# Softmax shifts of eight heads turned at once and put into the query stack by DMA, second attention pass thirteen heads behind the first

## What is computed

```python
xn = _adaln(x, cond, ln1_w, ln1_b)
q, k, v = split(xn @ qkv_w.T);  q, k = _rope(q), _rope(k)
x = x + _attn(q, k, v) @ sa_out_w.T              # layer 0: attention to itself
xn = _adaln(x, cond, ln2_w, ln2_b)
q = _rope(xn @ q_w.T);  k = _rope(ctx @ k_w.T);  v = ctx @ v_w.T
x = x + _attn(q, k, v) @ ca_out_w.T              # layer 1: attention to a context
xn = _adaln(x, cond, ln3_w, ln3_b)
x = x + gelu(xn @ ffn_w1.T + ffn_b1) @ ffn_w2.T + ffn_b2
# _attn: softmax(q k^T / sqrt(32)) v for each head
```

## Time and profile before

| what | value |
|---|---|
| median of 3 runs | 1967.09 us (1962.93 to 1968.1) |
| the profiled execution's own time | 1963.51 us |
| its span, first to last instruction | 1961.7 us |
| mean granted TensorE clock | 0.990 |
| PE busy | 1902.3 us, 97% |
| ACT, DVE, POOL busy | 1458.3, 1418.4, 783.0 us |
| attention block | from 0 to about 1278 us; first scores at about 50 us |
| feed-forward block | from about 1280 us to the end |

### The profile page before, as it was taken

The page is one execution under the profiler, slowest core; times in us unless marked ns, Lnnn a source line. Parts: engine busy times, 40 slices in busy tenths (PEclk is TensorE's granted clock), DMA queues, the critical chain, the costliest instruction groups (busy, mean ns, idle before and its releaser), DMA issues. The chain is left out here.

```text
span 1961.7 us, 39861 instructions
## 1 busy us (share of the span) xinstructions
PE 1902.3 (97%) x13588; PEld 1653.0 (84%) x13588; DVE 1418.4 (72%) x2509; ACT 1458.3 (74%) x4005; POOL 783.0 (40%) x820
## 2 busy tenths in 40 slices
PE   7899999999999999999999998899999999999999
PEld 6688888888887888888888877678899989898998
DVE  5777778778777887887887877645666666766654
ACT  3688888888888888888888888745666565665654
POOL 4334334334334444454453442013535354454531
PEclk9899999999999999999999999999999999999999
DMA  7867776876778677778778777343322313233130
GB/s 221 221 174 196 186 188 167 202 184 170 200 201 231 166 214 216 189 202 218 184 205 217 184 206 183 94 156 108 97 92 71 108 55 114 71 97 97 54 97 33
DMA packets 300197, 307.33 MB, mean 157 GB/s; under 512 B 15840, under 2 KB 253792, under 8 KB 300000
## 3 DMA queue, kind: packets, MB, share of 16 engines
q1 hardware_dynamic: 299408, 304.45, 57.4%
q10 hardware_dynamic: 592, 0.34, 0.1%
HBM read 212.46 MB, written 92.27 MB: 155 GB/s over the span
## 5 line engine op out<-in xcount | busy, mean ns | idle before, releaser
L738 ACT ACTIVATE ps_s<-ps_s,neg_max 128x256 f32<-128x256 f32 x1024 | 459.3, 451 | 85.1 <-DVE neg_max L853 81.6
L853 DVE TENSOR_REDUCE neg_max<-ps_s 128x2 f32<-128x512 f32 x512 | 352.7, 690 | 162.7 <-PE ps_s L607 158.8
L752 ACT ACTIVATE prob<-ps_s 128x512 f32<-128x512 f32 x512 | 304.6, 595 | 61.4 <-PE ps_s L627 58.1
L923 POOL TENSOR_TENSOR rope_c<-rope_c,rope_s 128x256 f32<-128x256 f32 x128 | 98.6, 770 | 425.2 <-DVE rope_s L834 425.2
L627 PE MATMUL ps_s<-qT,kT 104*128 104x256 f32 x1024 | 213.8, 291 | 21.0 <-ACT ps_s L738 6.4
L607 PE MATMUL ps_s<-kT,qT 96*128 96x256 f32 x1024 | 218.0, 295 | 10.7 <-DMA qT<-q_turned 5.4
L597 PE MATMUL ps_g<-xx_hi,w_hi 128*128 128x256 f32 x1024 | 214.3, 291 | 7.3 <-DVE rope_s L834 3.4
L607 PEld LDWEIGHTS ps_s<-kT,qT 96*128 96x128 f32 x1024 | 172.3, 193 | 54.8 <-ACT ps_s L738 19.4
L738 ACT ACTIVATION_READ_ACCUMULATOR ps_s<-ps_s,neg_max 128x1 f32 x1024 | 213.7, 209 | 0.0
L627 PEld LDWEIGHTS ps_s<-qT,kT 104*128 104x128 f32 x1024 | 168.8, 193 | 50.6 <-issue 19.4
L597 PE MATMUL ps_g<-xx_hi,w_lo 128*128 128x256 f32 x1024 | 207.6, 285 | 0.0
(11 more groups left out here) (155 smaller groups left out, 4826.9 us busy)
## 6 DMA issues: line engine op xcount, KB each, us to landing
kT<-k_turned SPq DMA_DIRECT2D x192, 256.0 KB, 5.3
qT<-q_turned SPq DMA_DIRECT2D x64, 512.0 KB, 7.3
f_raw<-in_w1T SPq DMA_DIRECT2D x124, 256.0 KB, 3.1
k_turned<-rot_hi SPq DMA_DIRECT2D x64, 256.0 KB, 4.5
k_turned<-rot_lo SPq DMA_DIRECT2D x64, 256.0 KB, 3.0
q_turned<-rot_hi SPq DMA_DIRECT2D x64, 256.0 KB, 4.6
q_turned<-rot_lo SPq DMA_DIRECT2D x64, 256.0 KB, 3.4
qT<-q_turned SPq DMA_DIRECT2D x64, 256.0 KB, 7.8
```

The source lines that it names most:

```text
L738: ins = eng.activation(scores[:, t * L:(t + 1) * L], scores[:, t * L:(t + 1) * L], ACT.Exp, bias=neg_max[G % 2][:, t, j:j + 1], accum_out= ...
L752: eng.activation(prob[:, n % NP, :, :].rearrange("p t l -> p (t l)"), ps_s[:, score_bank(step), :], ACT.Exp).then_inc(exp_done, 1)
L853: eng.tensor_reduce(neg_max[G % 2][:, :, j], ps_s[:, score_bank(step), :].rearrange("p (t l) -> p t l", l=L), AX.X, ALU.max, negate=True). ...
L923: eng.tensor_tensor(rope_c[n % 2][:, 0, :], rope_c[n % 2][:, 0, :], rope_s[:, 0, :], ALU.subtract)
```

## The change

- The turn is made once for eight heads (places 24 G + 24 to + 32 instead of twice per group), and its 16 rows are copied by ACT to a tile of their own, `max_rows`, two of them in turn.
- SP moves them into the query stack: two DMAs per eight heads (`max_rows`), one for the high and one for the low rows, 8 partitions to one partition each. `max_spread` goes away. The key stack needs only two rows of ones there (`ones`, a memset), and `pick` with its two loads goes away.
- LAG grows from 8 to 13. One fewer `prob` buffer is kept (9), and `mix` comes one head sooner after the last `weigh` of its eight.
- The stacks are filled four heads at a time (NQ = 6 places of four instead of 3 of eight), with twice as many DMAs of half the size.
- The copy of projected v from PSUM goes from ACT to DVE.
- In the table the projections of k, q, v and o move: o by 18 places later, q of layer 1 from p + 53 to p + 29 (turns of x there two places later), v from p + 29 and p + 46 to p + 42, and so on.

```diff
-LAG = 8
+LAG = 13
...
-            x_place = p + late + (31 if ahead == B else 16)
+            x_place = p + late + (31 if ahead == B else 18 if B < ahead < N else 16)
...
-                turns(shares((p + 29, 6, k[:4]), (p + 46, 7, k[4:])))
+                turns(spread(p + 29, 13, k))
...
-                    shares((p + 29, 6, v[:4]), (p + 46, 7, v[4:]))
+                spread(*((p + 42, 9, v) if ahead == B else (p + 42, 13, v)))
             if ahead < N - 1:
-                turns(spread(p + 53, 13, q))
+                turns(spread(*((p + 42, 13, q) if ahead < B else (p + 50, 10, q) if ahead == B else (p + 29, 13, q))))
...
-            spread(p + 37, 9, [("project", "o", i - 1, t, c) for cs in (range(KC - 1), (KC - 1,)) for t in range(T) for c in cs])
+            spread(p + 55, 9, [("project", "o", i - 1, t, c) for cs in (range(KC - 1), (KC - 1,)) for t in range(T) for c in cs])
...
-        for half in range(2):
-            put(24 * G + 12 * half + 12, "log", G, half)
-            put(24 * G + 12 * half + 13, "max_split", G, half)
-            put(24 * G + 12 * half + 19, "max_turn", G, half)
-            put(24 * G + 12 * half + 20, "max_copy", G, half)
-            put(24 * G + 12 * half + 23, "max_spread", G, half)
-        if G:
-            put(24 * G - 20, "stack", "k", G)
-            put(24 * G - 17, "stack", "q", G)
+        for n, kind in ((24, "log"), (25, "max_split"), (30, "max_turn"), (31, "max_copy"), (32, "max_rows")):
+            put(24 * G + n, kind, G)
+    for quad in range(2, 4 * N):
+        put(12 * quad - 20, "stack", "k", quad)
+        put(12 * quad - 17, "stack", "q", quad)
...
-        place = 3 * (8 * G + LAG + 9) + 2
+        place = 3 * (8 * G + LAG + 8) + 2
...
-                        if j % OH < 2:
-                            eng.wait_ge(maxes_spread if j % OH else maxes_copied, nth["max_turn", G, j // OH])
...
+                        if n % HG == 0:
+                            G = n // HG
+                            eng.wait_ge(max_rows_in[G % 2], 16 * 2 * (G // 2 + 1))
...
+                    elif kind == "max_rows":
+                        G = step[1]
+                        eng.wait_ge(maxes_copied, G + 1)
+                        if G >= NQ // 2:
+                            eng.wait_ge(weigh_done, HG * (G - NQ // 2 + 1))
+                        first = 2 * G % NQ
+                        for s in range(2):
+                            into = qT[ROWS + s:ROWS + s + 1, first:first + 2, :, :]
+                            eng.dma_start(into.rearrange("p g h l -> p (g h) l").bitcast(F32),
+                                          max_rows[G % 2][s * HG:(s + 1) * HG, :].bitcast(F32)).then_inc(max_rows_in[G % 2], 16)
```

More of the change, by code:

```diff
@@ L165, in stage_order @@
     yield ("warm", WARM_START)
-    yield ("pick",)
+    yield ("ones",)
     for h in range(2):
@@ L217, in stage_order @@
     yield from rotated("q", 0)
-    yield ("stack", "k", 0)
+    for quad in range(2):
+        yield ("stack", "k", quad)
     yield from (step for step in early if step[0] in turns_of_x)
@@ L221, in stage_order @@
     yield from rotated("k", 1)
-    yield ("stack", "q", 0)
+    for quad in range(2):
+        yield ("stack", "q", quad)
     yield from split("v", range(KC), "o")
@@ L384, in block_kernel @@
             total = [sb(f"total{n}", [P, T, HG]) for n in range(2)]
[L385 to L389, removed]
+            log_sb = sb("log_sb", [P, T, HG])
+            shift = sb("shift", [P, T, HG])
+            max_parts = sb("max_parts", [P, T, ROWS])
+            max_rows = [sb(f"max_rows{n}", [2 * HG, L], F32R) for n in range(2)]
+            NP = 9
             prob = sb("prob", [P, NP, T, L])
@@ L741, in attention_scalar @@
                     elif kind == "log":
-                        G, half = step[1:]
-                        eng.wait_ge(total_done, HG * G + OH * (half + 1))
-                        if nth[step] > 2:
-                            eng.wait_ge(shift_done, nth[step] - 2)
-                        eng.activation(log_sb[half][:, :, :], total[G % 2][:, :, OH * half:OH * (half + 1)], ACT.Ln).then_inc(log_done, 1)
+                        G = step[1]
+                        eng.wait_ge(total_done, HG * (G + 1))
+                        if G:
+                            eng.wait_ge(shift_done, G)
+                        eng.activation(log_sb[:, :, :], total[G % 2][:, :, :], ACT.Ln).then_inc(log_done, 1)
                     elif kind == "weigh":
@@ L812, in attention_vector @@
                                           ALU.subtract).then_inc(w_split, 1)
-                    elif kind == "pick":
-                        eng.wait_ge(small_in["pick"], 2 * 16)
-                        for r in range(NG):
-                            for half in range(2):
-                                eng.tensor_copy(kT[ROWS:MROWS, r, OH * half:OH * (half + 1), :],
-                                                pick_sb[ROWS:MROWS, :].unsqueeze(2).broadcast_to([2 * OH, OH, L])).then_inc(picked, 1)
+                    elif kind == "ones":
+                        eng.memset(kT[ROWS:MROWS, :, :, :].bitcast(F32), 1.0).then_inc(ones_set, 1)
                     elif kind == "project" and step[1] in "qk" and step[4] == KC - 1:
@@ L835, in attention_vector @@
                                           ALU.mult).then_inc(rope_taken, 1)
+                    elif kind == "project" and step[1] == "v" and step[4] == KC - 1:
+                        i, t = step[2:4]
+                        eng.wait_ge(product_done, products["v", i, t])
+                        if i >= NV and t == 0:
+                            eng.wait_ge(mix_done, KC * (i - NV + 1))
+                        eng.tensor_copy(v_sb[i % NV][:, t, :], ps_g[:, bank(("project", "v", i, t, 0)), :]).then_inc(v_done, 1)
                     elif kind == "project" and step[1] == "o" and step[4] == KC - 1:
@@ L990, in attention_sync @@
                     elif kind == "stack":
[L991 to L996 removed]
+                        m, quad = step[1:]
+                        i, n = divmod(quad, 4)
+                        eng.wait_ge(spilled[m][n // 2], 32 * (i + 1))
```

143 lines of the change are left out of this document (60 added, 83 removed).

## The result

The changed kernel takes **2096.13 us** (median of 4 runs, 2095.25 to 2096.9), the kernel before 1967.59 us on the same chip (1962.93 to 1969.89). The ratio is **1.0656 [1.0636, 1.0676]**: 6.6% slower, where 1930 us was forecast, with a range from 1904 to 1962. The profiled execution took 2096.90 us, its span is 2095.1 us, its mean granted clock 0.963 (before 0.990).

What follows compares the result with a forecast made beforehand. The prediction took PE, busy 97% of the span, as the bound. It summed -13.4 - 26 - 2 + 5 + 1.5 = -35 us against 1963.5 us to 1928.5, stated as 1930 us, range 1904 to 1962.

Steps and rivals of the forecast that it cites:

- Part 4: New wait of each eight heads' first `weigh` for the row DMAs: 0.08 us for each of 64, +5 us.
- The path of 2.6 + 0.6 + 2.0 = 5.2 us: From turn to rows in the query stack: ACT's copy ends after 2.6, SP's two issues 0.6 apart, landing 2.0 us.
- Time available, 7.4 us: From a turn to its first `weigh`, ten places later: 7.8 us, about 7.4 with the gains on PE.
- The slower rival: Row DMAs on SP's queue land 5.3 us from issue; each first `weigh` waits 1.1 us: 1994 us, chance 0.10.
- Its own sign: Wait of `weigh` on the row DMAs in the profile after: over 40 us in all.
- Part 1: Half of the turns on PE go: 64 pairs of transposes at 0.21 us each, -13.4 us.
- Part 2: ACT and DVE relieved, so PE waits less: half of the possible gain, 10.8 + 5.3 + 10.0, -26 us.
- The 5.3 us at the change of layers: Gain where the layers change, from PE's idle time and lower clock: half of 10.6 us.
- the 10 us of the late stretches: Gain in two late attention stretches, from PE's idle time and lower clock: half of 20.1 us.
- Part 3 and 5: Start, first scores needing four heads' stacks: -2 us; moved steps, five more `weigh` after the last scores: +1.5 us.
- The rule on small loads: Skill page's DMAs of at least 1 MiB: halved stack loads, one by one, would lose some 300 us; given little weight.
- the rival "small loads": Halved stack loads keep the DMA engines busy twice as long, costing 95 us: 2017 us, chance 0.02.

Runs made afterwards that it cites:

- e10: e7 with each max_turn's pair of transposes done twice, 128 more matmuls: 1953.68 us, ratio 0.9938 to the kernel before.
- e1: The change with `weigh` reading 96 rows, so not waiting for the row DMAs; softmax shift left out of the second pass: 1939.43 us, ratio 0.9848.
- e7: The change with the row DMAs issued by ACT instead of SP, both rows in one DMA: 1942.23 us, ratio 0.988 to the kernel before.
- e9: e7 with the statistics of the last x 8 places later: 1937.79 us, ratio 0.9853 to the kernel before.
- e11: e7 with 128 unused reductions of 0.94 us put on DVE at the old spreads' places: 1959.56 us, ratio 0.9958 to the kernel before.
- e5: The change with rows issued by ACT in two DMAs and the copy of v back on ACT: 1945.0 us, ratio 0.9893 to the kernel before.
- e12: e9 with the copy of v back on ACT: 1939.43 us, ratio 0.9853 to the kernel before.
- e6: The kernel before with only the copy of v moved from ACT to DVE: 1959.03 us, ratio 0.9966.

## Why the prediction was wrong

**The failed step is Part 4**: it left SP's time ahead of the rows out of the sum. The stack loads ahead were taken as "mostly through when ACT's copy ends", and of the spill it said: "In layer 0 a spill of q stands just ahead and may hold SP up. I add 0.08 us for each of 64". Neither got a duration, and that a spill of k stands ahead of the rows in layer 1 was not said. In the late cases SP needs 4.6 us of issue and 1.5 us at the spill between turn and rows in layer 0, and 2.5 and 2.2 us in layer 1. SP's stand at this spill was already in the trace of before, where no row DMA stood behind it:

```profile
SPq L987 <- POOL rot_lo L930: 251.2, 108, 5.3
```

The text put a price of 5 us on the whole wait. Measured, the first `weigh` starts some 120 us late in all, 1.9 us for each of 64, or 3.9 us for each of the 31 late ones, and the lower clock behind these waits adds some 56 us of slower matmuls, which the sum had no term for.

What else Part 4 said, by its own steps:

- *The path of 2.6 + 0.6 + 2.0 = 5.2 us* came out near the truth by luck, where SP is free. There, in the even turns of the steady part of layer 0, ACT's copy ends 1.5 us after the turn and not 2.6, and in the four of these turns in which PE waits, it starts 4.0 to 4.2 us after the first issue began, where 0.6 + 2.0 = 2.6 us was forecast: 5.5 to 5.8 us in all. The landing was priced some 1.4 us too low and the copy 1.1 us too high.
- *Time available, 7.4 us*: in the steady parts it is 7.2 us in the odd turns and 5.2 us in the even ones, in both layers, since a turn's ten places hold more or fewer projections. In layer 0 the late rows had the long distance, in layer 1 the short one, where even 4.9 us to the issue was far too late.
- The views shown of SP's order were the place of an even G in layer 0, where a spill stands *behind* the rows. The odd one, 24 places on, has it *ahead*. A step that recurs has to be looked at in each of its positions against the others' period; here that is two groups of eight in an item, in each layer.

**The slower rival** had the right consequence and the wrong mechanism. It said that the rows come late because they "land like the 256 KB loads", at 1.1 us each, all 64 of them, 1994 us. Where PE waits in the steady items it starts 3.2 to 4.4 us after the first of the two issues began, between the 2.6 us of the forecast and the 5.9 us of the rival; the rows are issued late, in 31 of the 64 cases, and by 3.9 us. Its own sign was over 40 us of wait, and 116.3 were found. Its chance, 0.10, was too low for a wait on the path whose DMAs stand in one queue with others that themselves wait.

**Part 1 was right**: 0.18 us measured per pair (e10) against 0.21.

**Part 2 was right in the steady part and not elsewhere.** Without the wait (e1) the change gains 30 us, where all parts but the fourth add up to 40, so the gains were put too high by 10. In e7 the periods are 36.40 us in layer 0 (440.67 less 404.27) and 35.65 in layer 1, forecast near 36.1 in both:

```profile
404.27 0.60 PE L566 MATMUL ps_g<-ident,xn 128*128 128x128 f32 x4
...
440.67 0.60 PE L566 MATMUL ps_g<-ident,xn 128*128 128x128 f32 x4
...
853.70 0.60 PE L566 MATMUL ps_g<-ident,xn 128*128 128x128 f32 x4
...
889.35 0.60 PE L566 MATMUL ps_g<-ident,xn 128*128 128x128 f32 x4
```

The waits on `total` from 112 to 575 us are 7.3 us in e9, half of the 14.8 in the earlier trace rows, as said:

```profile
PEld ps_s L603 <- ACT ps_s L732: 6.6, 16, 0.4
PEld ps_s L622 <- ACT ps_s L732: 0.7, 1, 0.7
```

DVE's part of it is measured by e11, 15 us; ACT's, by e5 and e12, is nothing once the spreads are gone (6.7 us with them, e6). So of "ACT's load falls only by some 3%, but the banks and the 0.95 us block on DVE go entirely" the block on DVE was the part that is shown to have paid; no run tests the banks alone. The 5.3 us at the change of layers did not come: the two items there take 46.5 + 40.0 us in e9 against 47.4 + 38.7. Nor did the 10 us of the late stretches: from the first `scores` of the third item from the end to the first matmul of the feed-forward block it is 129.0 us in e9, 129.6 before, and in e7, with the hole, 133.8. Some 5 us of the missing gain are that hole, a wait of DVE on a load in front of the split; for the rest no run here tells the cause.

**Part 3 and 5.** By the start of the fifth item e7 is 2.3 us ahead of the kernel before and e9 6.1, two kernels that are the same up to there; so the start gained something, and its 2 us can't be told from this scatter. The moved q projections cost nothing that shows: in layer 1 no wait of q on x appears, as was said.

**The rule on small loads.** The halved loads did not cost DMA time, they landed sooner: in the change 2.9 us for 128 KB of k in the median where 256 KB took 5.3, and 3.0 us in e9.

```profile
kT<-k_turned SPq DMA_DIRECT2D x384, 128.0 KB, 2.9
qT<-q_turned SPq DMA_DIRECT2D x128, 256.0 KB, 3.7
```

Over the whole program the queue that carries them moved 304.5 MB both before and in e9, in 57.4% of the DMA engines' time before and in 52.5% in e9, whose span is also shorter:

```profile
q1 hardware_dynamic: 299408, 304.45, 57.4%
```

```profile
q1 hardware_dynamic: 304528, 304.47, 52.5%
```

The Trainium skill's page "DMA: Bandwidth & Descriptors", section "Bandwidth", asks for 1 MiB and more for each DMA; by that rule these loads should have lost. The 2.0 us a DMA of the prediction's estimate stands in another section of that page, "Anatomy of one DMA — SWDGE (gpsimd) path", for DMAs that GpSimd issues, and these are issued by SP. The measurement decides: with several loads under way at once, 128 KB each is no loss in this kernel, and the rival "small loads" (chance 0.02) is refuted. What the smaller loads do cost is SP's time, 0.6 us for each of five more issues in eight heads, and that time stands in front of the rows. How the change would do with loads of eight heads and the rows on SP, no run tells.

## What to carry to other kernels

A DMA on the path belongs in a queue in which nothing ahead of it can wait, best on the engine that writes its source; before placing it, walk the issuing engine's list through a whole period and put a time on each wait and each issue ahead of it (here the issues were the larger part in both layers). Price a new wait at each of its positions, and add the slower clock behind it. And work that nobody waits for still costs where it stands in front of something that is waited for: 0.94 us on a DVE that is 67% busy was worth 0.12 us of PE.

## What was not expected of the hardware

- The wait cost half again as much as it lasted: 103.5 us more idle time on PE and 52.6 us more busy time for the same matmuls, at a mean clock of 0.963 instead of 0.989.
- An issue on SP takes 0.70 us (median) for the rows, 8 KB in 8 pieces, 0.59 to 0.62 for a stack load of 128 KB, and 0.38 for a load of 256 KB of feed-forward weights: the cost does not follow the bytes. Both rows in one DMA took 0.69 us once, and not twice.
- Rows of 8 KB from one place of SBUF to another were usable 3.2 to 4.4 us after the first of the two issues began (3.4 us in the case shown, with the DMA engines half busy), which is longer than a 128 KB load of k took to land, 2.9 us in the median.
